# Moving the attention slots around a group's two additions, with operand units transposed when they are made

## The reference

```
x = x + 0.5 * ffn(layernorm(x), W1, W2, W3)
x = x + attn(layernorm(x), qkv_w, qkv_norm_w, proj_w, proj_norm_w, norm_w, s)
x = x + 0.5 * ffn(layernorm(x), W1, W2, W3)

ffn(x)  = fwht(silu(x @ W1.T) * (x @ W3.T)) @ W2.T          # 2048 hidden, Walsh-Hadamard over them
attn(x): h = rmsnorm(x) ; q, k, v = h @ ternary(qkv_w).T    # 16 heads of 32
  per chunk of 128 tokens, state S per head:
    o = scale * ((q k^T * decay mask) v + q * lam_t @ S) ; S = lam_T * S + (k * lam_rev)^T v
  out = rmsnorm(rmsnorm(o)) @ ternary(proj_w).T
```

## Time and profile before

| | |
|---|---|
| time, median of two runs | 2593.06 us (2589.89 to 2596.24) |
| the profiled execution | 2601.9 us, of which the span from first to last instruction 2600.2 us |
| TensorE busy, and its weight loads | 2323.7 us (89%), 1479.4 us |
| VectorE busy | 1537.3 us (59%) |
| ScalarE busy | 882.9 us (34%) |
| GpSimd busy | 495.1 us (19%) |
| mean granted TensorE clock | 0.963 |
| forked part, 658 to 2600 us | TensorE busy 1728.66 of 1942 us |

### The profile page before, as it was taken

The page is one execution under the profiler, slowest core; times in us unless marked ns, Lnnn a source line. Parts: engine busy times, 40 slices in busy tenths (PEclk is TensorE's granted clock), DMA queues, the critical chain, the costliest instruction groups (busy, mean ns, idle before and its releaser), DMA issues.

```text
span 2600.2 us, 41818 instructions
## 1 busy us (share of the span) xinstructions
PE 2323.7 (89%) x16307; PEld 1479.4 (57%) x16307; DVE 1537.3 (59%) x2904; ACT 882.9 (34%) x1568; POOL 495.1 (19%) x702
## 2 busy tenths in 40 slices
PE   7999989989578898899888988899988998999899
PEld 3444444434355566566555656567656665666676
DVE  6587566666265655666566456755676466446533
ACT  6545233233132333233323323233233322332222
POOL 0270222122111111112111111111121211111120
PEclk9999999999799999999999999999999999999999
DMA  7955765555945646557465375655755445464552
GB/s 196 230 138 156 192 166 132 135 140 135 164 130 144 172 110 138 153 141 163 133 162 164 97 173 139 155 150 124 179 156 136 145 111 158 117 142 119 135 135 65
DMA packets 445955, 378.96 MB, mean 146 GB/s; under 512 B 322240, under 2 KB 368320, under 8 KB 443456
## 3 DMA queue, kind: packets, MB, share of 16 engines
q1 hardware_dynamic: 397472, 218.44, 35.6%
q0 software_dynamic: 48000, 157.32, 21.8%
q10 hardware_dynamic: 288, 0.52, 0.1%
HBM read 223.09 MB, written 77.59 MB: 116 GB/s over the span
## 4 chain that ended last, share of the span: by engine, by line
PE 50%; DVE 19%; DMA 12%; issue 8%; SPq 4%; ACT 4%; POOL 2%; DVEq 0%; ACTq 0%; POOLq 0%
PE d_bank L1921 12%; PE d_bank L1902 11%; PE g_bank L1902 6%; PE a_bank L1953 4%; DMA work<-parts_dram 3%; PE l_bank L1902 3%; DMA unit_dram<-cent 3%; PE d_bank L1855 3%; PE a_bank L1936 2%; PE a_bank L2012 2%; PE g_bank L1835 2%; PE l_bank L1835 2%; DVE stat L1561 1%; DVE work L1735 1%; ACT work L1226 1%
## 5 line engine op out<-in xcount | busy, mean ns | idle before, releaser
L1902 PE MATMUL d_bank<-work,w1t 128*128 128x256 f16 x3456 | 432.7, 284 | 139.6 <-DVE w1t L1414 58.6
L1921 PE MATMUL d_bank<-w2t,work 128*128 128x512 f16 x2304 | 539.5, 385 | 2.1 <-DVE work L1279 2.1
L919 POOL DMA_DIRECT2D w1t<-sum_dram x480 | 262.1, 546 | 1323.4 <-PE d_bank L1902 1102.0
L1902 PEld LDWEIGHTS d_bank<-work,w1t 128*128 128x128 f16 x3456 | 344.0, 101 | 225.3 <-issue 162.7
L1921 PEld LDWEIGHTS d_bank<-w2t,work 128*128 128x128 f16 x2304 | 225.5, 99 | 249.6 <-issue 14.6
L1443 DVE SCALAR_TENSOR_TENSOR w3t<-d_bank,table,w3t 128x512 f32<-128x512 f32 x188 | 140.7, 748 | 370.9 <-PE d_bank L1921 370.3
L1170 ACT CAST work<-w3t 128x512 f16<-128x512 f32 x192 | 118.6, 618 | 367.7 <-DVE w3t L1428 220.3
L1855 PE MATMUL d_bank<-w2t,work 128*128 128x512 f16 x636 | 150.4, 392 | 16.7 <-DVE work L1526 11.6
L1226 ACT CAST work<-work 128x512 f16<-128x512 f32 x128 | 79.1, 618 | 242.9 <-DVE work L1735 242.0
L1902 PE MATMUL g_bank<-xt,w1t 128*128 128x256 f16 x1152 | 151.2, 284 | 11.1 <-DMA xt<-unit_dram 11.1
L1902 PE MATMUL l_bank<-xt,w1t 128*128 128x256 f16 x1152 | 144.6, 276 | 4.6 <-DMA xt<-unit_dram 4.6
(11 more groups left out here) (301 smaller groups left out, 3303.1 us busy)
## 6 DMA issues: line engine op xcount, KB each, us to landing
w1t<-sum_dram POOLq DMA_DIRECT2D x480, 256.0 KB, 3.2
work<-parts_dram SPq DMA_DIRECT2D x192, 128.0 KB, 3.8
unit_dram<-cent SPq DMA_DIRECT2D x72, 256.0 KB, 2.6
x_dram<-work SPq DMA_DIRECT2D x12, 1024.0 KB, 4.5
parts_dram<-q_parts SPq DMA_DIRECT2D x32, 256.0 KB, 2.0
parts_dram<-k_parts SPq DMA_DIRECT2D x32, 256.0 KB, 3.2
w3t<-x_dram POOLq DMA_DIRECT2D x16, 512.0 KB, 5.3
w2t<-in_L_ffn_W_dram SPq DMA_DIRECT2D x30, 256.0 KB, 3.4
```

The lines of the kernel that those rows point to most:

```text
L919: nc.gpsimd.dma_start(ring[arg % RING], sum_dram[mat, chunk % CHUNKS, unit].rearrange("p q k a h -> p (q k a h)")).then_inc(ring_landed[ar ...
L1902: ins = nc.tensor.matmul(dst[:, HALF_T * q:HALF_T * (q + 1)].rearrange("p (i t) -> p i t", i=2), weights, x_unit[:, :, xp, k, :], start=(n ...
L1921: ins = nc.tensor.matmul(d_bank[2 + i % 2][:], hid_s[:, 2 * m + half, hp, cols], w2t[:, j, wp, :], start=(m == 0 and q == 0 and hp == wp), ...
```

## The change

```diff
-        RING = 7
+        RING = 5
...
-                    steps += product(mat, 1) + product(mat, 5)
-                    if n == FORKED and c == mat == 0:
-                        steps += [("begin", n - 1), ("down", HT - 1)] + [("resid", t) for t in range(TT)]
-                    steps += slot(6 * mat) + slot(6 * mat + 1) + part(0) + slot(6 * mat + 2)
-                    steps += product(mat, 6) + product(mat, 2) + slot(6 * mat + 3) + part(1) + slot(6 * mat + 4)
-                    steps += product(mat, 7) + product(mat, 3)
+                    if mat == 0:
+                        steps += product(0, 1) + product(0, 5)
+                        if n == FORKED and c == 0:
+                            steps += [("begin", n - 1), ("down", HT - 1)] + [("resid", t) for t in range(TT)]
+                        steps += slot(0) + part(0) + slot(1)
+                    else:
+                        steps += product(1, 1) + slot(6) + product(1, 5) + slot(7) + part(0) + slot(8) + slot(9)
+                    steps += product(mat, 6) + product(mat, 2) + part(1) + product(mat, 7) + product(mat, 3)
                     if c == 0 and n > FORKED:
                         steps += [("rows", (n, mat))]
-                    steps += product(mat, 4) + ([("lows", chunk)] if mat else []) + slot(6 * mat + 5)
+                    if mat == 0:
+                        steps += slot(2) + slot(3) + product(0, 4) + slot(4) + slot(5)
+                    else:
+                        steps += slot(10) + product(1, 4) + [("lows", chunk)] + slot(11)
...
-                return ([[("stat", key)]] + [[(step, (key, i))] for i in range(2) for step in ("uprep", "umix", "ulow")])
+                return [[("stat", key)], [("uprep", (key, 0))], [("umix", (key, 0)), ("uturn", (key, 0))],
+                        [("ulow", (key, 0)), ("uprep", (key, 1)), ("uturn", (key, 1))],
+                        [("ustore", (key, 0)), ("umix", (key, 1)), ("uturn", (key, 2))], [("ustore", (key, 1))],
+                        [("ustore", (key, 2)), ("ulow", (key, 1)), ("uturn", (key, 3))]]
...
+                if unit_norm(key):
+                    add(slots, at + len(norm_steps(key)) + 1, [("ustore", (key, 3))])
+                    if key[0] == "ffn1" and key[1] > FORKED:
+                        add(slots, at - 4, [("xload", key[1])])
...
-                at = SUM_SLOT + 3 * i if i < EARLY_SUMS else LATER_SUM_SLOT + 3 * (i - EARLY_SUMS)
+                at = SUM_SLOT + 3 * i if i < EARLY_SUMS else LATER_SUM_SLOTS[i - EARLY_SUMS]
...
-        SUM_SLOT, LATER_SUM_SLOT = -14, 49
+        SUM_SLOT, LATER_SUM_SLOTS = -15, (49, 52, 55, 58, 66, 69, 72, 75, 78, 81, 84, 87, 90)
...
+        def wide_halves(key, k, b):
+            if k % 2 == 0:
+                return halves[:, b].rearrange("p a d -> p (a d)")
+            if key == ("ffn2", 0):
+                return at["qs"].bitcast(F16)[:, 2 * D * b:2 * D * (b + 1)]
+            return w1t[:, 1, 1 + b, HALF_H:H]
+
+        def turned_home(key, k, b):
+            if key == ("ffn2", 0):
+                return at["ks" if k % 2 else "sc"].bitcast(F16)[:, 2 * D * b:2 * D * (b + 1)]
+            return xin[:, k % 2 + 2 * b, :].bitcast(F16)
...
-                    sp.dma_start_transpose(operand[u].rearrange("p (e t) -> p e t", t=P),
-                                           unit_dram[nf, unit].rearrange("p i e -> p (i e)")).then_inc(operand_landed[u], 16)
+                    sp.dma_start(operand[u], unit_dram[nf, unit].rearrange("p i e -> p (i e)")).then_inc(operand_landed[u], 16)
+                elif step == "uturn":
+                    key, k = arg
+                    sp.wait_ge(u_lo, 8 * UNIT[key] + 2 * (k + 1))
+                    past = 2 * UNIT[key] + k // 2
+                    if past:
+                        sp.wait_ge(u_stored[k % 2], 32 * past)
+                    sp.wait_ge(ln_norm, TT * NORM[key] + (2 if k == 0 else TT))
+                    for b in range(2):
+                        cols = D if k % 2 == 0 and b else 2 * D
+                        sp.dma_start_transpose(turned_home(key, k, b)[:, 0:cols].rearrange("p (e t) -> p e t", t=P),
+                                               wide_halves(key, k, b)[:, 0:cols]).then_inc(u_flipped[k % 2], 16)
...
+                elif step == "ustore":
+                    key, k = arg
+                    nf, i = ORDER.index(key), k // 2
+                    pool.wait_ge(u_flipped[k % 2], 32 * (2 * UNIT[key] + k // 2 + 1))
+                    for b in range(2):
+                        turned = turned_home(key, k, b)
+                        if k % 2 == 0 and b:
+                            nc.gpsimd.dma_start(unit_dram[nf, 2, :, i, :], turned[:, 0:D]).then_inc(u_stored[0], 16)
...
```

More of the change, by code:

```diff
@@ L125, in macaron_kernel @@
         spare = at["yt"][:, 3 * D:4 * D]
[L128 removed]
+        SUMS, EARLY_SUMS = 2 * (HT // 2) * 2, 19
         sum_extra = sb("sum_extra", [P, 2, P])
@@ L257, in macaron_kernel @@
         u_hi, u_lo, u_mixed = sem("u_hi"), sem("u_lo"), sem("u_mixed")
+        u_flipped = [sem("u_flipped0"), sem("u_flipped1")]
         u_stored = [sem("u_stored0"), sem("u_stored1")]
@@ L342, in forked_feed_forward @@
                 for i, name in enumerate(PRODUCTS):
-                    steps += [("operand", (n, name)), ("ring", i)]
+                    steps += [("operand", (n, name))] + ([("ring", i)] if i < RING else [])
                 steps += [("rows", (n, 0)), ("rows", (n, 1))]
@@ L736, in _ @@
                     for b in range(2):
[L737 removed]
+                        sp.wait_ge(u_stored[b], 32 * 2 * (UNIT[ORDER[nf]] + 1))
                     unit = {1: 0, 5: 3, 6: 6, 2: 1, 7: 5, 3: 2, 4: 4}[name]
[L739 to L757 removed]
@@ new lines, in _ @@
+                    sp.dma_start(operand[u], unit_dram[nf, unit].rearrange("p i e -> p (i e)")).then_inc(operand_landed[u], 16)
[6 more added lines that the diff above has]
+                    sp.wait_ge(ln_norm, TT * NORM[key] + (2 if k == 0 else TT))
+                    for b in range(2):
+                        cols = D if k % 2 == 0 and b else 2 * D
+                        sp.dma_start_transpose(turned_home(key, k, b)[:, 0:cols].rearrange("p (e t) -> p e t", t=P),
+                                               wide_halves(key, k, b)[:, 0:cols]).then_inc(u_flipped[k % 2], 16)
+                elif step == "xload":
+                    sp.wait_ge(ln_norm, TT * NORM["ffn1", arg])
+                    for side in range(2):
+                        sp.wait_ge(u_stored[side], 32 * 2 * UNITS_DONE["ffn1", arg])
+                    sp.dma_start(xin[:], x_tiles[bass.ds(arg * TT, TT)].rearrange("t p d -> p t d")).then_inc(x_loaded, 16)
@@ L917, in _ @@
                         pool.wait_ge(p_done, product_at(used // 2, used % 2, SUMMED[k]))
+                    if chunk < CHUNKS and i == 0:
+                        pool.wait_ge(sum_stored, 16 * SUMS // CHUNKS * (chunk + 1))
                     unit = {5: 3, 6: 0, 7: 2, 3: 1, 4: 4}[SUMMED[i]]
@@ L937, in _ @@
                                  sum_turned(i).rearrange("p u a d -> p u (a d)")).then_inc(sum_stored, 16)
+                elif step == "ustore":
[6 more added lines that the diff above has]
+                            nc.gpsimd.dma_start(unit_dram[nf, 2, :, i, :], turned[:, 0:D]).then_inc(u_stored[0], 16)
+                        else:
+                            units = slice(3 + 2 * b, 5 + 2 * b) if k % 2 else slice(0, 2)
+                            nc.gpsimd.dma_start(unit_dram[nf, units, :, i, :].rearrange("u p e -> p u e"),
+                                                turned.rearrange("p (u e) -> p u e", u=2)).then_inc(u_stored[k % 2], 16)
                 elif step == "qmean":
@@ L1096, in _ @@
                         act.wait_ge(u_mixed, 2 * UNIT[key] + i + 1)
+                    past, later = 2 * UNIT[key] + i, step == "ulow"
+                    if past:
+                        act.wait_ge(u_flipped[later], 32 * past)
                     for b in range(2):
-                        past = 4 * UNIT[key] + 2 * i + (step == "ulow")
-                        if past:
-                            act.wait_ge(u_stored[b], 16 * past)
                         if step == "uprep" and i == 0:
                             act.wait_ge(flipped[b], 16 * 2 * PLAIN_DONE[key])
-                        parts = halves[:, b].rearrange("p a d -> p (a d)").rearrange("p (u a d) -> p u a d", u=2, a=2)
+                        elif later and key == ("ffn2", 0):
+                            act.wait_ge(q_moved, 16 * BLOCKS * GROUPS)
+                            act.wait_ge(a_ready[0], filled("score", (0, GROUPS - 1, TT - 1))[1])
+                        elif later:
+                            act.wait_ge(g_ready, HT * FORKED)
+                        parts = wide_halves(key, 2 * i + later, b).rearrange("p (u a d) -> p u a d", u=2, a=2)
                         if step == "uprep" and b == 1:
@@ L1676, in _ @@
```

(2 more changed lines are left out.)

22 lines of the change are left out of this document (2 added, 20 removed).

## The result

The changed kernel takes 2703.97 us (median of two runs, 2702.1 to 2705.83) against 2593.06 us. The ratio is 1.0428, with a 95% interval of 1.0365 to 1.0491. The profiled execution has a span of 2704.1 us against 2600.2, so 103.9 us have to be found. The forecast was 2620 us with a range up to 2680: the sign of the sum was right, its size was not, and the range missed.

What follows compares the result with a forecast made beforehand. TensorE's gaps, 276.5 us, with 137.3 us of addition waits in the forked part; +74 odd groups, +18 even, -28 `halves`, -11 seam, -25 norms = +28 us, 2620 us as the median; range 2530 to 2680.

Steps and rivals of the forecast that it cites:

- odd groups, DMA waits of the score: Batches 1, 3, 5: k's 12.4 us chain outlasts the products left; 8.5 us stall in eight groups, 68 us, plus 3.
- new chain of scores, odd and even groups: Scores one product apart wait for VectorE: 1.5 us ten times in odd groups, 3.2 us 16 times in even ones.
- additions beside `halves` and in the groups gone: Product 4's three stalls of 7.09 to 8.97 us go, as do addition waits of 7 us (odd) and 3.7 us (even).
- the other norms: o, ffn2 and qkv norms in seven batches: 103 us of addition waits mostly return elsewhere, a quarter saved, -25 us.
- operand and ring waits at the seams: First forked layer: plain loads cut 18.7 us of waits to 7.5, -11 us; other seams and ring of five nothing.
- moved sums: Rescheduled weight sums end where they did; no cost entered in the sum.
- slow clock: After odd stalls the next twelve matmuls run at the lower clock level: 8 x 1.25 = 10 us.
- Rival A: Additions stand free, nothing else takes the waits, the odd stall stays: -96 us, 2497 us as the median; chance 0.22.
- Rival B: Odd groups' score decides and norms' waits return as `forked` and `s_lo`: +78 us, 2671 us; chance 0.22.
- Rival C: Product 4 still waits over 1 us on average for the second addition: +64 us, 2657 us; chance 0.06.
- two signs that were to show the forecast wrong: k's chain under 9 us when queues are free of operand transposes, or even batches' `forked` and `part` waits over 60 us.
- The stalls on `halves`: Low halves get own buffers, so product 4's three long stalls and the slow clock after them go: -28 us.

Runs made afterwards that it cites:

- experiment 2: The kernel before with only the new slot places: 2704.13 us, ratio 1.0446.
- experiment 3: The changed kernel with mat 0's slots laid out like mat 1's: 2651.8 us, ratio 1.0231 to the kernel before.
- experiment 9: The changed kernel with k's projection, parts and DMAs one slot earlier in batches 1, 3 and 5, except first groups: 2657.55 us, ratio 1.0232 to the kernel before.
- experiment 1: The changed kernel with the slots back in their old places, all else kept: 2598.78 us, ratio 1.0028 to the kernel before.
- experiment 7: The kernel before with only the change's schedule of the weight sums: 2609.95 us, ratio 1.0049.
- experiment 8: The changed kernel with old slot places and old sums, keeping turned units, own buffers and ring of five: 2597.21 us, ratio 0.999 to the kernel before.
- experiment 4: The changed kernel with a unit norm's third store on POOL moved behind the next norm's power: 2697.55 us, ratio 1.0414 to the kernel before.

## Why the prediction was wrong

Against the forecast's sum of +28 us (profiled), the measured one is +104.

| step of the prediction | forecast | measured |
|---|---|---|
| odd groups, DMA waits of the score: new, less their old 15 | +71 - 15 | 68.4 in nine waits, old ones gone: +53 |
| even batches' old DMA waits gone | -29 | -29, all eleven |
| new chain of scores, odd and even groups | +15 + 51 | 43.5 (14.6 and 29), less 7.1 before: +36 |
| additions beside `halves` and in the groups gone | -24 - 7 - 4 | -34, no second addition waits |
| **the other norms** | **-25** (bounds -80, +25) | **+41** |
| operand and ring waits at the seams | -11 | 14.9 for 18.6: -4 (first seam 3.17, last 7.55) |
| idle time ahead of the forked part (moved sums and else) | 0 | +15 |
| TensorE's busy time (slow clock), less the `halves` stalls' 4 | +10 - 4 | +23 |
| small waits, not listed | 0 | +3 |
| sum | +28 | +104 |

**The step that failed** is "The other norms ... I take a quarter off". The prediction had 103 us of addition waits that belong to norms, had counted the new order by hand, found "about as much as before, in another wait", set +25 as the bound, and then chose -25 because the second addition would no longer catch them. The trace of after has 69.6 (first addition) + 22.2 (fork) + 19.7 (part) + 35.3 (turned norm) = 146.8 us; 3.1 us of such waits were there before, so 143.7 us stand against the 78 that the sum had, 66 us more. That all of it belongs to norms is read from where the waits stand, not from a run that takes them away. The hand count was the better estimate and even it was too low. Even batches' statistics in front of product 6 had 7.7 us in the prediction against 5.2 of cover, which leaves 2.5, and the wait at 1063.77 (and three like it) is 3.98. What it lacked above all was a norm's last tile: in an even batch the last `split` stands in slot 4 and the first q projection in slot 7; between them there were products 7, 3, 4, 1 and 5, and now there are 1 and 5 alone. Four projections waited 8.82, 6.75, 12.88 and 6.87 us (5.68, 4.82, 4.42 and 4.68 with the places alone, in experiment 2; the rest comes with the other parts of the change). The prediction read only the waits that existed (the additions) and asked whether they would go; that product work had stood *between a norm's transposes and their use* was never written down as cover, though for k's DMAs the same question was asked and answered well.

In the layouts that were run, none won the 110 us: with a slot's work before the first addition (experiment 3), before the second (the kernel before) or before the next score (the changed kernel) something else waits. Rival A (the additions stand free and nothing takes the waits) needed the opposite. Rival B's mechanism is in the measured profile, at a higher price than its 78 us; beside the fork and the low parts that it named, it is the first addition and the turned norm that wait. Rival C is refuted: product 4 waits for no second addition. Of the two signs that were to show the forecast wrong neither pointed at the loss: k's chain was under 9 us in four of nine groups (8.3 to 8.9), but that only shortens a stall, and fork and part waits were 41.9 us, under 60. The waits that grew most, of the first addition and for the turned norm, had no sign.

**The second term of note** is the clock. The forecast had eight times 1.25 us for runs of matmuls at the lower level. TensorE's busy time grew by 22.8 us, and shrank again to 2333.5 us with the odd stalls gone (experiment 9) and to 2318.4 with the old places (experiment 1). So of the 28 us that the places put on busy time, 13 go with the odd stalls; the rest must lie with the other stalls, which the forecast had not charged with any clock, though no run isolates it.

**The even chain** was over-costed by 22 us, and by 7 more since the like waits of before (7.1 us) were not taken off. VectorE's chain was right: 8.1 us from kv to the last pv, forecast 8.3. TensorE's work beside it was too low: 5.1 us in the sum, 8.1 - 1.81 = 6.3 in the trace. **The moved sums** were put at 0 because they "end where they did"; experiment 7 has 12.6 us for them. **The odd groups** were right in cause, place and size: 8.5 us each for eight groups, and their mean is 8.3. The Trainium skill ("DMA: Bandwidth & Descriptors", Anatomy of one DMA) would have put an odd stall at some 4.5 us, by a fit that it gives for the GpSimd path, while SP issues these DMAs; the trace's 8.3 us disagree with that estimate after the change too.

**The plain operand loads**: they land in 4.2 us where the transposed ones took 4.9, and the first seam's products wait 3.17 us in place of 18.7; with the old sums, where TensorE isn't late for it, 7.80 (experiment 8), close to the 7.5 of the forecast. But experiments 1 and 8 have the whole of this part at 1.0028 and 0.999. What the Trainium skill says against it ("Advanced Engine Details and Errata", X-Bar Transpose: as fast as regular DMAs) is nearer to that result than the prediction's -11 us, though by the landing times a difference is there. What the first seam wins in experiment 8, two later ones lose (5.5 and 4.3 us), and the sum had them at nothing. **The stalls on `halves`** went as forecast, but with the old places others took their room (experiment 8), so their 28 us are not a gain that any run shows.

Together: +28, +66 for the norms, +15 ahead of the forked part, +17 for busy time, +7 at the seams, -30 for the chain of scores, -3 for the score's DMA and +3 of small waits is +103, against +104.

## What to carry to other kernels

Here, moving work away from the wait at which it showed moved the wait: before pricing the move, list for every moved step who uses its result next, how much other work stood between and how much is left, for transposes and reloads as well as for k's chain. When a hand count and a hopeful discount disagree, take the count. The gain here lay in the reverse move: a short step (k's low part, 0.68 us) ahead of a long DMA chain, issued one slot earlier, gave 1% together with the turned units that alone gave nothing, and only in the forked part.

## What the runs showed of the hardware

A relayout through DRAM (256 KB stored, a transpose, six 128 KB loads) took 8.3 to 13.5 us from VectorE's last write to the first matmul. Its length varies with how late the loads land: 3.7 us at the median of the run, 7.9 us in the stretch from 1880 to 1900 us, 7.3 us in that from 1787 to 1801. What makes them late there was not isolated.

After a stall of 11.54 us TensorE's next part shows 4.79 us instead of 2.75, at a granted clock of 0.57 (1.00 before the stall), for the most part the lower of its two levels (1.2 for 2.4 GHz); in experiment 9, 60 us less of such waits took 13 us off TensorE's busy time too.

A short instruction on POOL pays for the DMA issues in front of it: the power of 1.03 us at 1134.77 stood behind a 5.34 us wait for a turn and two issues of 0.71 and 0.58 us, though its input was ready at 1129.89. With one of the stores moved behind it (experiment 4) the stall of TensorE fell from 12.42 to 8.11 us.
